# FFN weights transposed by VectorE in 32x32 blocks, in a fused gated cross-attention and FFN layer

## The chip, the cores and the metric

One core of one Trainium2 chip. The metric is the device time of one launch in microseconds (us), the median of several runs; lower is better. The engines are named PE (TensorE matmul), PEld (its weight load), DVE (VectorE), ACT (ScalarE), POOL (GpSimd) and SP (SyncE, which here only issues transfers).

## The reference

Everything is float32. x and the context are 8 batches of 128 tokens by 512.

```
x = x + tanh(g_xattn) * attention(layernorm(x), context)   # 32 heads, 8 key/value heads, D = 128, rotary positions, mask
x12 = layernorm(x) @ w12.T + b12                            # w12 is 1024 x 512, rows are outputs
x1, x2 = split(x12)                                         # 512 each
x = x + tanh(g_ffn) * ((silu(x1) * x2) @ w3.T + b3)         # w3 is 512 x 512
```

Both FFN weights are stored with outputs as rows, so the contraction axis lies along a row. The tensor engine needs it on the partitions: twelve tiles of 128x512 (eight of w12, four of w3) have to be transposed.

## The kernel before

Each float32 operand is carried as two parts, hi and lo (the rounded value and the rest), and each product is three matmuls: hi by hi, lo by hi, hi by lo (lines 468 to 470 on PE). ACT makes the hi part of a tile (L806), and DVE (L1211) or POOL (L1072) subtracts it from the source to get the lo part.

The attention runs in 32 pairs, named (gg, c) with gg 0 to 3 and c 0 to 7, p = 8 gg + c; a pair is two batches (k = 0 and 1) of one group of four heads. For each k the chain is: `scores` on PE (L591, L592) into s_banks; `mask_scores` on DVE (L1337, then four L1346), which frees s_banks; `exps` on ACT (L876, four); `recip` on DVE (L1356); `norm` on POOL (L1114); `prob_transpose` on PE (L474) into t_bank; `pT_hi_copy` on ACT and `pT_lo_split` on DVE; `pv` on PE into pv_bank; `o_hi_copy` on ACT and `o_lo_split` on DVE; `out_proj` on PE into o_bank[k]; and `add_out` on DVE (L1370), which adds to `resid`. Pairs up to (3,4) also hold two `q_block`s each, the query projections of later pairs, with which PE has other work while these chains run. The last three pairs, (3,5) to (3,7), have none.

Each engine works through its own list in order and waits on counting semaphores. The lists of pairs (3,5) to (3,7) and of what follows are written out by hand. There the layer norm of the FFN begins on DVE (`h_stats`, then the Newton steps of the inverse square root, L1225 to L1241, each of which waits for the one before), ACT normalises (`h_norm`), PE transposes the result (`h_tile`), and ACT and DVE split it (`h_copy`, `h_lo`). `up(half, m)` is the first FFN product, `down(half, b)` the second.

The twelve weight tiles are loaded by SP with one transfer each (L455), rows on partitions. `ffn_tile(t)` on PE is four 128x128 transposes through the identity into f_bank. `ffn_tile_copy(t)` on ACT copies that bank to a stage (t_cos or t_sin) and makes the hi part from the stage, `ffn_tile_lo(t)` on POOL makes the lo part. Tiles 0 to 7 stand among the instructions of pairs (3,5) to (3,7), tiles 8 and 9 after `out_proj(3,7,1)`, ahead of the first `up`, and tiles 10 and 11 between the first two `up`s.

Of the kernel before, what the change touches and what calls it, by code (L numbers as in the profile page):

```python
# [75 lines left out]
def build(nc, x, ctx, pos, mask, g_x, g_f, Wq, Wk, Wv, Wo, w12, b12, w3, b3, out):  # L76
# [1469 lines left out]
```

## Time and profile before

| | |
|---|---|
| median of 3 runs | 674.37 us (674.37 to 674.54) |
| the profiled execution | 674.48 us |
| its span | 672.7 us, so 1.8 us lie around it |
| PE busy | 661.8 us, 98%; granted clock 1.00 throughout |
| DVE, ACT, POOL busy | 482.4 us (72%), 322.0 us (48%), 385.6 us (57%) |
| chain that ended last | 90% PE, 4% DVE, 2% ACT |

A matmul's row shows its own duration, which overlaps with the next one's; what an operation takes of PE's time is read from the distance between starts. Times are from the start of the span.

### The profile page before, as it was taken

Reading aid. Unit: us, or ns where it says so; the run is one execution under the profiler, and the core shown is the slowest. Engines: PE = TensorE matmul, PEld = TensorE weight load, DVE = VectorE, ACT = ScalarE, POOL = GpSimd, SP = SyncE. Lnnn points to the kernel's source line nnn. Section 1 sums busy time; section 2 is a strip of 40 time slices with the busy share of each in tenths; the row PEclk is TensorE's granted clock in tenths of the full one; section 3 lists DMA queues with packets and bytes.
Section 4 is the critical chain, followed back from the end, with each engine's and each line's share of the span. In section 5 each row is a group of like instructions: output and inputs, shape, how many; then the busy total and the mean of one; then the engine's idle time right before and its main releaser. Section 6 shows DMA issues by size and latency. Waiting matters only on the chain.

```text
span 672.7 us, 11338 instructions
## 1 busy us (share of the span) xinstructions
PE 661.8 (98%) x3357; PEld 554.3 (82%) x3357; DVE 482.4 (72%) x1223; ACT 322.0 (48%) x903; POOL 385.6 (57%) x323
## 2 busy tenths in 40 slices
PE   8999999999999999999999999999999999999998
PEld 7888888788888888888888888888888887778886
DVE  3987666877777777777777777777777777774433
ACT  4336613554554544554554544554554537756210
POOL 6457757966666666656666666556666655631000
PEclk9999999999999999999999999999999999999999
DMA  9996982331213121321212120321211142000002
GB/s 304 317 318 215 304 295 94 142 100 58 95 39 104 32 94 33 109 71 55 94 43 98 33 94 31 110 79 45 78 33 31 32 157 80 0 1 1 1 31 95
DMA packets 62157, 66.34 MB, mean 99 GB/s; under 512 B 5920, under 2 KB 43808, under 8 KB 62112
## 3 DMA queue, kind: packets, MB, share of 16 engines
q1 hardware_dynamic: 60688, 64.77, 29.5%
q0 software_dynamic: 384, 1.05, 0.4%
q8 instruction: 18, 0.29, 0.2%
q14 instruction: 27, 0.22, 0.1%
q10 hardware_dynamic: 1040, 0.00, 0.1%
HBM read 46.93 MB, written 18.87 MB: 98 GB/s over the span
## 4 chain that ended last, share of the span: by engine, by line
PE 90%; DVE 4%; ACT 2%; issue 1%; POOL 1%; DMA 1%; SPq 0%; DVEq 0%; ACTq 0%
PE f_bank L468 11%; PE f_bank L470 11%; PE f_bank L469 11%; PE o_bank L468 9%; PE o_bank L470 9%; PE o_bank L469 9%; PE s_banks L591 6%; PE t_bank L474 4%; PE pv_bank L468 4%; PE pv_bank L470 3%; PE pv_bank L469 3%; PE s_banks L592 2%; PE t_bank L468 1%; PE t_bank L470 1%; PE t_bank L469 1%
## 5 line engine op out<-in xcount | busy, mean ns | idle before, releaser
L1114 POOL TENSOR_TENSOR prob<-prob,small 128x512 f32<-128x512 f32 x64 | 66.7, 1042 | 134.5 <-DVE small L1356 134.5
L876 ACT ACTIVATE prob<-prob,small 128x128 f32<-128x128 f32 x256 | 99.8, 391 | 80.3 <-DVE small L1346 74.9
L468 PE MATMUL o_bank<-wo_hi,o_hi 128*128 128x512 f32 x256 | 105.7, 413 | 0.0
L806 ACT ACTIVATE o_hi<-pv_bank 128x512 fp32r<-128x512 f32 x64 | 38.4, 599 | 138.1 <-PE pv_bank L470 137.7
L468 PE MATMUL f_bank<-xT_hi,wq_hi 128*128 128x512 f32 x256 | 101.5, 396 | 0.0
L470 PE MATMUL o_bank<-wo_hi,o_lo 128*128 128x512 f32 x256 | 100.5, 393 | 0.0
L469 PE MATMUL o_bank<-wo_lo,o_hi 128*128 128x512 f32 x256 | 100.0, 391 | 0.0
L1072 POOL TENSOR_TENSOR q_lo<-q,q_hi 128x512 fp32r<-128x512 f32 x64 | 82.7, 1292 | 30.0 <-ACT q_hi L806 30.0
L470 PE MATMUL f_bank<-xT_hi,wq_lo 128*128 128x512 f32 x256 | 99.8, 390 | 0.0
L469 PE MATMUL f_bank<-xT_lo,wq_hi 128*128 128x512 f32 x256 | 99.8, 390 | 0.0
L1258 DVE TENSOR_TENSOR t_sin<-f_bank,rope 64x512 f32<-64x512 f32 x128 | 88.2, 689 | 2.8
L1105 POOL TENSOR_TENSOR q<-t_cos,t_sin 128x512 f32<-128x512 f32 x64 | 82.9, 1295 | 1.0 <-DVE t_sin L1258 0.9
L1258 DVE TENSOR_TENSOR t_cos<-f_bank,rope 128x512 f32<-128x512 f32 x64 | 43.9, 687 | 32.1 <-PE f_bank L470 32.0
L1346 DVE CUSTOM_DVE_ANT_0 prob<-s_banks,prob 128x128 f32<-128x128 f32 x256 | 59.2, 287 | 10.2 <-DVE prob L1337 7.1
L591 PE MATMUL s_banks<-k_parts,q_hi 128*128 128x256 f32 x256 | 63.0, 324 | 0.7 <-issue 0.4
L1370 DVE SCALAR_TENSOR_TENSOR resid<-o_bank,small,resid 128x512 f32<-128x512 f32 x64 | 47.9, 749 | 19.6 <-PE o_bank L470 18.6
L1211 DVE TENSOR_TENSOR o_lo<-pv_bank,o_hi 128x512 fp32r<-128x512 f32 x64 | 44.1, 689 | 20.9 <-ACT o_hi L806 20.8
L470 PEld LDWEIGHTS o_bank<-wo_hi,o_lo 128*128 128x128 f32 x256 | 48.0, 188 | 11.0
L592 PE MATMUL s_banks<-k_parts,q_lo 128*128 128x128 f32 x256 | 56.9, 222 | 0.0
L470 PEld LDWEIGHTS f_bank<-xT_hi,wq_lo 128*128 128x128 f32 x256 | 48.0, 188 | 10.2
L468 PEld LDWEIGHTS f_bank<-xT_hi,wq_hi 128*128 128x128 f32 x256 | 48.1, 188 | 9.5 <-issue 0.4
L469 PEld LDWEIGHTS f_bank<-xT_lo,wq_hi 128*128 128x128 f32 x256 | 48.2, 188 | 9.1
(176 smaller groups left out, 1463.3 us busy)
## 6 DMA issues: line engine op xcount, KB each, us to landing
k_scratch<-ks_parts SPq DMA_DIRECT2D x16, 512.0 KB, 3.2
raw<-in_L_xattn_Wq_dram SPq DMA_DIRECT2D x32, 256.0 KB, 2.7
raw<-in_L_xattn_Wo_dram SPq DMA_DIRECT2D x32, 256.0 KB, 2.7
k_parts<-k_scratch SPq DMA_DIRECT2D x16, 512.0 KB, 3.7
v_scratch<-vs_hi SPq DMA_DIRECT2D x16, 256.0 KB, 3.9
v_scratch<-vs_lo SPq DMA_DIRECT2D x16, 256.0 KB, 3.9
v_hi<-v_scratch SPq DMA_DIRECT2D x16, 256.0 KB, 3.9
v_lo<-v_scratch SPq DMA_DIRECT2D x16, 256.0 KB, 4.4
```

The source lines that it names most:

```text
L468: nc.tensor.matmul(dst, st[0], mv_[0], start=start, stop=False)
L469: nc.tensor.matmul(dst, st[0], mv_[1], start=False, stop=False)
L470: return nc.tensor.matmul(dst, st[1], mv_[0], start=False, stop=stop)
L591: nc.tensor.matmul(s_banks[:, 256 * h:256 * (h + 1)], q_hi[:, k, h, :], k_parts[:, half, b, :], start=True, stop=False)
L592: mm = nc.tensor.matmul(s_banks[:, 256 * h:256 * h + 128], q_lo[:, k, h, :], k_parts[:, half, b, 0:128], start=False, stop=True)
L876: e = nc.scalar.activation(prob[:, k, h, :], prob[:, k, h, :], ACT.Exp, bias=nmin[k][:, h:h + 1], scale=-1.0, accum_out=psum_row[k][:, h:h ...
L1072: nc.gpsimd.tensor_tensor(dst, a, b_, ALU.subtract).then_inc(s, 1)
L1105: nc.gpsimd.tensor_tensor(q32[:, (e // 4) % 2, e % 4, :], t_cos[:, ts, :], t_sin[:, ts, :], ALU.add).then_inc(pool_rope, 1)
L1114: nc.gpsimd.tensor_tensor(prob[:, k], prob[:, k], rrow[k].unsqueeze(2).to_broadcast([128, GH, S]), ALU.mult).then_inc(pool_norm, 1)
L1258: return nc.vector.tensor_tensor(dst, a, b_, ALU.mult)
L1346: op = nc.vector.tensor_tensor_reduce(prob[:, k, h, :], s_parts[:, h, 0, :], prob[:, k, h, :], 1.0, HUGE, ALU.add, ALU.min, nmin[k][:, h:h ...
L1370: nc.vector.scalar_tensor_tensor(out=resid[:, b, :], in0=o_bank[k][:, :], scalar=tg_x, in1=resid[:, b, :], op0=ALU.mult, op1=ALU.add).then ...
```

## The change

The tensor engine's twelve `ffn_tile`s go, and ACT's copy to a stage with them. SP loads each tile with four transfers instead of one. Each moves 32 partitions, and each partition receives four pieces of 128 elements from four rows of the weight, chosen so that a transpose inside each 32x32 block gives the full transpose. `ffn_tile(t)` is now one DVE instruction over 128x512 (`nc.vector.transpose`), from SBUF to SBUF. ACT's `ffn_hi(t)` is one copy from its result, POOL's `ffn_lo(t)` one subtraction as before. The order of features on the partitions is a permutation, so `h_norm` writes its result permuted in the same way, and b12 is loaded in that order (eight transfers, now late in the kernel instead of at its start).

PE's order in the attention is the same without the tiles. Banks have moved: `up` uses f_bank and s_banks; `h_tile` 0 to 3 use the two halves of s_banks in turn, so `h_tile(2)` and `(3)` each wait for the split (`h_copy`, `h_lo`) of the tile two before; the outputs of pair (3,6) go to f_bank, so that `out_proj(3,7,1)` doesn't wait for an o_bank. On ACT, POOL and DVE, the lists from pair (3,2) on are written out anew. The bodies of these lists are cut here to a line or two.

```diff
-        w12_hi = cT_lo
-        w12_lo = place("w12_lo", [128, KT, TOK], F32R, at["wo_hi"])
+        w12_hi = place("w12_hi", [128, RAW, KT, 128], F32R, at["raw"])
+        w12_lo = place("w12_lo", [128, RAW, KT, 128], F32R, at["cT_lo"])
+        w12_all = place("w12_all", [128, RAW, KT, 128], F32, at["cT_lo"])
+        w3_all = place("w3_all", [128, KT, E], F32, at["wq_lo"])
...
-        up_bank = [s_banks[:, 0:512], s_banks[:, 512:1024], t_bank[:, :], pv_bank[:, :]]
+        up_bank = [f_bank[0][:, :], f_bank[1][:, :], s_banks[:, 0:512], s_banks[:, 512:1024]]
...
         def h_bank(b):
-            return (f_bank[0], f_bank[1], t_bank, s_banks[:, 0:512], *f_bank, *f_bank)[b]
+            s0, s1 = s_banks[:, 0:512], s_banks[:, 512:1024]
+            return (s0, s1, s0, s1, t_bank, pv_bank, *o_bank)[b]
+
+        def ffn_src(t, i):
+            f = slice(128 * i, 128 * i + 128)
+            if t < RAW:
+                return w12.rearrange("(h j m b) f -> h m b j f", h=2, j=4, m=4)[t % 2, t // 2, :, :, f]
+            return w3.rearrange("(t j b) f -> t b j f", t=4, j=4)[t - RAW, :, :, f]
...
-                sp.dma_start(dst, src).then_inc(s, 16)
+                for i in range(4):
+                    sp.dma_start(dst[32 * i:32 * i + 32, :].rearrange("b (j f) -> b j f", j=4), ffn_src(t, i)).then_inc(s, 16)
...
-            def ffn_tile(t):
-                src, loaded, count = ffn_tile_src(t)
-                pe.wait_ge(loaded, count)
...
-                transpose4(f_bank[t % 2], lambda k: src[:, k * 128:(k + 1) * 128]).then_inc(pe_ftile, 1)
...
             def h_tile(b):
                 pe.wait_ge(act_xn, B + b + 1)
                 if b < 2:
-                    pe.wait_ge(act_fstage, 7 + b)
-                elif b == 2:
+                    pe.wait_ge(dve_mask, 8 * KVH)
+                elif b < 4:
+                    tiles_done(H_T + b - 2)
+                elif b == 4:
...
-            for b in range(4):
-                h_tile(b)
+            h_tile(0)
+            h_tile(1)
+            h_tile(2)
+            h_tile(3)
             out_proj(3, 7, 1)
-            ffn_tile(8)
-            ffn_tile(9)
-            tiles_done(H_T + 3)
             up(0, 0)
-            ffn_tile(10)
-            ffn_tile(11)
             up(0, 1)
...
-            def ffn_tile_copy(t):
-                act.wait_ge(pe_ftile, t + 1)
...
-                hi(ffn_stage(t), f_bank[t % 2][:, :], act_fstage)
-                act.wait_ge(act_fstage, t + 1)
-                hi(ffn_tile_dst(t, 0), k4(ffn_stage(t)), act_fhi)
+            def ffn_hi(t):
+                act.wait_ge(dve_ftile, t + 1)
+                hi(ffn_parts(t)[0], ffn_f32(t), act_fhi)
...
+            exps(3, 7, 0)
             pT_hi_copy(3, 7, 0)
+            h_norm(0)
             exps(3, 7, 1)
...
+            def ffn_tile(t):
+                src, loaded, count = ffn_raw(t)
+                dve.wait_ge(loaded, count)
...
+                nc.vector.transpose(ffn_f32(t).rearrange("p k (j b) -> p k j b", j=4), src.rearrange("p (j k a) -> p k j a", j=4, k=4)).then_inc(dve_ftile, 1)
```

Three places of the new lists, as they stand before and now. The first is VectorE between `recip(3,7,0)` and the mask of `scores(3,7,1)`. Before (RECIPROCAL is `recip`, the resid row is `add_out(3,6,0)`, the last row begins the mask):

```order
L1211 TENSOR_TENSOR o_lo<-pv_bank,o_hi 128x512
L1214 BN_STATS small<-resid 128x6
L1216 BN_AGGR small<-small 128x2
L1356 RECIPROCAL small<-small 128x4
L1370 SCALAR_TENSOR_TENSOR resid<-o_bank,small,resid 128x512
L1337 TENSOR_TENSOR prob<-s_banks,mfill 128x512
```

Now:

```order
L1451 RECIPROCAL small<-small 128x4
L1326 SCALAR_TENSOR_TENSOR small<-small 128x4
L1327 TENSOR_TENSOR small<-small 128x4
L1328 SCALAR_TENSOR_TENSOR small<-small 128x4
L1326 SCALAR_TENSOR_TENSOR small<-small 128x4
L1327 TENSOR_TENSOR small<-small 128x4
L1328 SCALAR_TENSOR_TENSOR small<-small 128x4
L1336 SCALAR_TENSOR_TENSOR small<-small 128x4
L1432 TENSOR_TENSOR prob<-s_banks,mfill 128x512
```

Six Newton steps and the shift have come in between, all with both inputs in SBUF; `add_out(3,6,0)` has gone behind.

The second is GpSimd from `q_lo_split(3,7,1)` on: prob rows are `norm(3,7,0)` and `norm(3,7,1)`, w_lo rows are lo parts of weight tiles. Before:

```order
L1072 TENSOR_TENSOR q_lo<-q_61,q_hi 128x512
L1114 TENSOR_TENSOR prob<-prob,small 128x512
L1072 TENSOR_TENSOR w_lo<-t_cos,cT_lo 128x4x128
L1114 TENSOR_TENSOR prob<-prob,small 128x512
L1072 TENSOR_TENSOR w_lo<-t_sin,cT_lo 128x4x128 x2
```

Now:

```order
L1143 TENSOR_TENSOR q_lo<-q_61,q_hi 128x512
L1185 TENSOR_TENSOR prob<-prob,small 128x512
L1143 TENSOR_TENSOR w_lo<-w_all,w_hi 128x512 x3
L1185 TENSOR_TENSOR prob<-prob,small 128x512
L1143 TENSOR_TENSOR wq_lo<-w_all,wq_hi 128x4x128 x4
```

Three tiles instead of one stand between the two norms.

The third is VectorE at the start of pair (3,5), around the mask of `scores(3,5,1)`. Before, `o_lo_split(3,4,1)` stands ahead of it:

```order
L1211 TENSOR_TENSOR o_lo<-pv_bank,o_hi 128x512
L1356 RECIPROCAL small<-small 128x4
L1370 SCALAR_TENSOR_TENSOR resid<-o_bank,small,resid 128x512
L1337 TENSOR_TENSOR prob<-s_banks,mfill 128x512
L1346 ISA prob,small<-s_banks,prob 128x128
```

Now:

```order
L1451 RECIPROCAL small<-small 128x4
L1432 TENSOR_TENSOR prob<-s_banks,mfill 128x512
L1441 ISA prob,small<-s_banks,prob 128x128
L1441 ISA small 128x1
L1441 ISA prob,small<-s_banks,prob 128x128
L1441 ISA small 128x1
L1441 ISA prob,small<-s_banks,prob 128x128
L1441 ISA small 128x1
L1441 ISA prob,small<-s_banks,prob 128x128
L1441 ISA small 128x1
L1306 TENSOR_TENSOR o_lo<-pv_bank,o_hi 128x512
L1532 STREAM_TRANSPOSE w_all<-ffn_raw_95 128x4x128
```

`o_lo_split(3,4,1)` now stands behind the whole mask, and behind it one of the new transposes.

## Rows read from the trace of the kernel before

**Rows 1.** Groups by line and shape, TensorE, 555 to 615 us: busy us, mean ns; idle before

```profile
L474 PE MATMUL f_bank<-ident,raw 128*128 128x128 f32 x32 | 4.6, 275 | 0.0
...
L474 PE MATMUL f_bank<-ident,ffn_raw 128*128 128x128 f32 x16 | 2.1, 272 | 0.0
```

**Rows 2.** Timeline, TensorE: start us, duration us, instruction, idle before it

```profile
544.32 0.45 PE L468 MATMUL f_bank<-xT_hi,wq_hi 128*128 128x512 f32 x1
...
547.11 0.60 PE L474 MATMUL t_bank<-ident,prob 128*128 128x128 f32 x4
...
559.41 0.61 PE L474 MATMUL f_bank<-ident,raw 128*128 128x128 f32 x4
...
564.77 0.66 PE L474 MATMUL t_bank<-ident,prob 128*128 128x128 f32 x4 [0.23 <-POOL prob L1114]
...
571.73 0.62 PE L474 MATMUL f_bank<-ident,raw 128*128 128x128 f32 x4
...
576.90 0.66 PE L474 MATMUL t_bank<-ident,prob 128*128 128x128 f32 x4 [0.66 <-POOL prob L1114]
...
579.07 0.47 PE L468 MATMUL pv_bank<-pT_hi,v_hi 128*128 128x512 f32 x1
...
583.85 0.62 PE L474 MATMUL f_bank<-ident,raw 128*128 128x128 f32 x4
...
589.02 0.66 PE L474 MATMUL t_bank<-ident,prob 128*128 128x128 f32 x4 [0.68 <-POOL prob L1114]
...
590.02 0.47 PE L468 MATMUL o_bank<-wo_hi,o_hi 128*128 128x512 f32 x1
...
600.02 1.03 PE L474 MATMUL f_bank<-ident,ffn_raw 128*128 128x128 f32 x8
600.82 0.47 PE L468 MATMUL s_banks<-xT_hi,cT_lo 128*128 128x512 f32 x1
```

**Rows 3.** Timeline, VectorE, the last pairs and the end of the attention

```profile
557.27 0.69 DVE L1211 TENSOR_TENSOR o_lo<-pv_bank,o_hi 128x512 fp32r<-128x512 f32 x1
...
571.93 0.69 DVE L1337 TENSOR_TENSOR prob<-s_banks,mfill 128x512 f32<-128x512 f32 x1 [0.42 <-PE s_banks L592]
...
573.67 0.69 DVE L1211 TENSOR_TENSOR pT_lo<-t_bank,pT_hi 128x512 fp32r<-128x512 f32 x1
...
578.22 0.69 DVE L1211 TENSOR_TENSOR pT_lo<-t_bank,pT_hi 128x512 fp32r<-128x512 f32 x1 [0.42 <-ACT pT_hi L806]
...
582.82 0.18 DVE L1356 RECIPROCAL small<-small 128x4 f32<-128x4 f32 x1 [0.61 <-ACT prob L876]
...
584.05 0.69 DVE L1337 TENSOR_TENSOR prob<-s_banks,mfill 128x512 f32<-128x512 f32 x1 [0.42 <-PE s_banks L592]
...
598.24 0.68 DVE L1211 TENSOR_TENSOR xT_lo<-f_bank,xT_hi 128x512 fp32r<-128x512 f32 x1
```

**Rows 4.** Timeline, ScalarE, 597 us

```profile
597.56 0.60 ACT L806 ACTIVATE xT_hi<-t_bank 128x512 fp32r<-128x512 f32 x1
```

**Rows 5.** Timeline, GpSimd, 583 us

```profile
583.08 1.04 POOL L1114 TENSOR_TENSOR prob<-prob,small 128x512 f32<-128x512 f32 x1 [0.27 <-DVE small L1356]
```

**Rows 6.** Timeline, VectorE, 42 to 45 us

```profile
42.62 1.18 DVE L1231 SCALAR_TENSOR_TENSOR small<-small 128x8 f32<-128x8 f32 x1
43.84 1.21 DVE L1232 TENSOR_TENSOR small<-small 128x8 f32<-128x8 f32 x1
45.08 0.17 DVE L1233 SCALAR_TENSOR_TENSOR small<-small 128x8 f32<-128x8 f32 x1
```

**Rows 7.** Timeline, GpSimd, the same stretch

```profile
42.48 1.29 POOL L1072 TENSOR_TENSOR ks_parts<-k,ks_parts 128x512 fp32r<-128x512 f32 x1 [0.74 <-ACT ks_parts L806]
43.74 1.28 POOL L1072 TENSOR_TENSOR wk_lo<-raw,wk_hi 128x512 fp32r<-128x512 f32 x1
```

**Rows 8.** Groups by line and shape, VectorE: times, busy us, mean ns; idle before

```profile
L1214 DVE BATCH_NORM_STATS2 small<-resid 128x6 f32<-128x512 f32 x16 | 11.0, 690 | 0.3
```

**Rows 9.** Busy us by engine in pair (3,3): window, PE, PEld, DVE, ACT, POOL

```profile
525.64:540.73 15.09, 15.09 (x80) 12.77 (x78) 11.60 (x33) 7.04 (x23) 9.18 (x8) 1.00 0.11 36
```

More of the change, by code:

```diff
@@ L52 @@
 FFN_TILES = 12
+LATE = 3
 WARM = 8
@@ L674, in _ @@
                     pair(gg, c)
-            for c in range(1, 5):
+            for c in range(1, LATE):
                 pair(3, c)
@@ L728, in down @@
                 mm.then_inc(pe_down, 1)
+            q_block(3, 12)
+            scores(3, 3, 1)
+            q_block(3, 13)
+            prob_transpose(3, 3, 0)
+            out_proj(3, 2, 0)
+            pv(3, 3, 0)
+            prob_transpose(3, 3, 1)
+            out_proj(3, 2, 1)
+            scores(3, 4, 0)
+            pv(3, 3, 1)
+            q_block(3, 14)
+            scores(3, 4, 1)
+            q_block(3, 15)
+            prob_transpose(3, 4, 0)
+            out_proj(3, 3, 0)
+            pv(3, 4, 0)
+            prob_transpose(3, 4, 1)
+            out_proj(3, 3, 1)
+            scores(3, 5, 0)
+            pv(3, 4, 1)
             out_proj(3, 4, 0)
             scores(3, 5, 1)
-            ffn_tile(0)
             prob_transpose(3, 5, 0)
@@ L780, in _ @@
             up(0, 3)
-            tiles_done(H_T + 7)
             up(1, 0)
@@ L973, in _ @@
                     pair(gg, c)
-            for c in range(1, 5):
-                pair(3, c)
+            pair(3, 1)
             def h_norm(b):
@@ new lines, in _ @@
+            ffn_tile(2)
+            mask_scores(3, 3, 0)
+            ffn_tile(3)
+            ffn_tile(4)
+            recip(3, 3, 0)
+            mask_scores(3, 3, 1)
+            o_lo_split(3, 2, 1)
+            add_out(3, 1, 1)
+            cos_q(3, 12)
+            recip(3, 3, 1)
+            cos_q(3, 13)
+            pT_lo_split(3, 3, 0)
+            ffn_tile(5)
+            add_out(3, 2, 0)
+            sin_q(12)
+            pT_lo_split(3, 3, 1)
+            o_lo_split(3, 3, 0)
+            sin_q(13)
@@ new lines, in _ @@
+            mask_scores(3, 4, 0)
+            ffn_tile(6)
+            add_out(3, 2, 1)
+            cos_q(3, 14)
+            recip(3, 4, 0)
+            mask_scores(3, 4, 1)
+            sin_q(14)
+            o_lo_split(3, 3, 1)
+            cos_q(3, 15)
+            recip(3, 4, 1)
+            pT_lo_split(3, 4, 0)
+            ffn_tile(7)
+            add_out(3, 3, 0)
+            ffn_tile(8)
+            o_lo_split(3, 4, 0)
+            pT_lo_split(3, 4, 1)
+            ffn_tile(9)
+            mask_scores(3, 5, 0)
@@ new lines, in _ @@
+            sin_q(15)
+            add_out(3, 3, 1)
+            recip(3, 5, 0)
+            mask_scores(3, 5, 1)
+            o_lo_split(3, 4, 1)
+            ffn_tile(10)
+            recip(3, 5, 1)
+            add_out(3, 4, 0)
+            pT_lo_split(3, 5, 0)
+            h_stats(0)
+            add_out(3, 4, 1)
+            o_lo_split(3, 5, 0)
+            pT_lo_split(3, 5, 1)
+            mask_scores(3, 6, 0)
+            o_lo_split(3, 5, 1)
+            ffn_tile(11)
+            recip(3, 6, 0)
@@ new lines, in _ @@
+            h_stats(1)
+            mask_scores(3, 6, 1)
+            add_out(3, 5, 0)
+            pT_lo_split(3, 6, 0)
+            h_stats(2)
+            recip(3, 6, 1)
+            add_out(3, 5, 1)
+            o_lo_split(3, 6, 0)
+            h_stats(3)
+            pT_lo_split(3, 6, 1)
+            mask_scores(3, 7, 0)
+            o_lo_split(3, 6, 1)
+            inv_std_begin(0, 4, NEWTON_OPS)
+            newton_step(0, 4, NEWTON_OPS, 0)
+            recip(3, 7, 0)
+            newton_step(0, 4, NEWTON_OPS, 1)
@@ new lines, in _ @@
+            newton_step(0, 4, NEWTON_OPS, 2)
+            shifts(0, 4)
+            mask_scores(3, 7, 1)
+            pT_lo_split(3, 7, 0)
+            recip(3, 7, 1)
+            o_lo_split(3, 7, 0)
+            add_out(3, 6, 0)
+            h_stats(4)
+            pT_lo_split(3, 7, 1)
+            add_out(3, 6, 1)
+            o_lo_split(3, 7, 1)
+            h_lo(0)
+            h_lo(1)
+            add_out(3, 7, 0)
+            h_lo(2)
+            h_lo(3)
+            h_stats(5)
+            add_out(3, 7, 1)
```

411 lines of the change are left out of this document (237 added, 174 removed).

## The prediction

> **What bounds the kernel now.** I read the page first. PE is busy 98% of the span and holds 90% of the chain that ended last, so PE's time is the price of everything. The question is whether the time taken from PE is time that it needs, or time in which it waits anyway. For that I read the groups by line around the end of the attention, then PE's timeline pair by pair, then the engines that PE waits for.
>
> The groups show what goes: 48 transposes of 128x128, 6.7 us of busy time [rows 1]. By distance between starts it is less. Tiles 8 and 9 take 600.82 - 600.02 = 0.80 us together; at 0.40 to 0.46 a tile, twelve are 5.1 us [rows 2].
>
> The timeline shows where PE waits. Call S(c) the end of `scores(3,c,1)` and T(c) the start of `prob_transpose(3,c,1)`. Then T(5) - S(5) = 564.77 - 559.41 = 5.36, T(6) - S(6) = 5.17 and T(7) - S(7) = 5.17, each T with an idle time in front, released by POOL's norm [rows 2]. This stretch is a latency: mask, exps, recip, norm. The mask starts 0.20 after S and takes 1.74 (571.93 to 573.67) [rows 3]; PE's transpose comes 4.97 after the mask's start (584.05 to 589.02) [rows 2, 3]. With less work on PE it does not get shorter.
>
> **The change part by part.** The sum is made against the profiled execution, 674.48 us with a span of 672.7, 0.1 above the median of 674.37.
>
> *Tiles 0 to 7 off PE.* Tiles 0, 3 and 6 stand between S and T, so they fill a wait: worth nothing by themselves. Tiles 1, 2, 4 and 5 stand between T(c) and `pv(3,c,1)`. That product needs `pT_lo`, which starts 1.32 after T (578.22) and takes 0.69, so it can't start before T + 2.1; it does at T + 2.17 (579.07) [rows 2, 3]. Again the tiles fill a wait. Tile 7 stands between T(7) and `out_proj(3,7,0)`, which starts at T(7) + 1.0 (590.02) [rows 2]. There ACT's two copies for a tile delayed the o split, so with them gone out_proj can follow at T(7) + 0.4. Pair (3,6) gets some 0.1 longer or shorter by small moves of h_stats and the copies; I take +0.1.
>
> *The end of the attention, T(7) to the first `up`.* Before, this is 600.82 - 589.02 = 11.80 [rows 2]. Now: out_proj from 0.4 to 3.25 and pv to 3.95; `h_tile` 0 and 1 to 4.85. `h_tile(2)` has to wait until pv's result is split and `h_copy(0)` and `h_lo(0)` are through. ACT's two copies (0.5 to 0.6 each) bring it to 5.3, DVE's o split and h_lo (0.6 to 0.69 each) to 6.15 [rows 3, 4]. `h_tile(3)` waits for the next h_lo, to 6.85, and ends at 7.25; out_proj(3,7,1), 2.8, ends at 10.05. Tiles 8 and 9 no longer follow. Gain 1.75, in which tile 7 and tiles 8 and 9 are contained.
>
> *Tiles 10 and 11.* They lie between two `up`s of a PE that is busy throughout, and the layer norm and gates ahead of later `up`s have more than 2 us of room: gain 0.8, as for tiles 8 and 9.
>
> *Pair (3,5).* `o_lo_split(3,4,1)` now follows the mask of `scores(3,5,1)`. So `out_proj(3,4,1)` starts at S(5) + 0.20 + 1.74 + 0.69 + 0.1 = S + 2.75; with its 2.8 and pv's 0.7, T(5) comes at S + 6.25, against 5.36 before [rows 2, 3]: loss 0.9.
>
> *Pair (3,4).* POOL does `q_lo_split(3,5,1)` ahead of `norm(3,4,0)`. ACT's copy for it can only start when scores(3,4,1) are done; 0.2, 0.6 for ACT, 1.25 for POOL and 1.04 for the norm are 3.1, while PE has one q_block, 547.11 - 544.32 = 2.79 [rows 2, 4, 5, 7]: loss 0.3.
>
> *Pair (3,7), the largest term.* Six Newton steps and the shift stand on DVE between `recip(3,7,0)` and the mask of scores(3,7,1), all with two inputs in SBUF. At the same time POOL has norm(3,7,0), which starts 0.26 after recip (583.08 against 582.82), and now three tiles' lo parts behind it, all ready [rows 3, 5]. What that does can be read at 42 us. A Newton step that takes 0.17 took 1.18 there and ended at 43.80, as POOL's subtraction ended at 43.77; the next took 1.21, ending at 45.05 with POOL's next; with POOL idle the one after took 0.17 [rows 6, 7]. One small step passes for each POOL instruction. So, from R, the start of recip: POOL is busy from R + 0.26 to 1.3 (norm), then 3 x 1.25 to R + 5.04. Step 1 passes; steps 2 to 5 end with the four POOL instructions, the last at R + 5.05; two more at 0.2 each, and the mask starts at R + 5.5. Without the block it would be R + 1.5, which is just S(7) + 0.2, as before. Everything in front of T(7) hangs behind this mask: PE waits, and T(7) is 3.95 later.
>
> The Trainium skill, in "SBUF — State Buffer", section "Who interferes with whom", says that a VectorE instruction with two SBUF inputs and a GpSimd one that reads SBUF exclude each other for the whole instruction; the trace agrees, with 1.18 and 1.21 us in place of 0.17, and by the rule the norm and `scalar_tensor_tensor` block as well. The same section says that one with a single SBUF input outside the two-port modes does not contend; by it the new transposes would not wait for POOL. No row here shows a transpose.
>
> *The DVE transposes.* The nearest row is the instruction that reads 128x512 from SBUF alone, 0.69 us [rows 8]; I take it. The lower end is the same row less the 0.1 in which neighbours overlap, 0.6; the upper end is 0.69 plus a blocked wait of 1.2, some 1.9 [rows 6]. Ten of them fall into pairs (3,2) to (3,5), where a pair of 15.09 us leaves DVE 15.09 - 11.60 = 3.5 idle [rows 9], over three pairs 10.5. At 0.65 a slot they take 6.5: hidden behind PE's q_blocks. At 1.9 they take 19, and 3 to 8 us come onto PE. The two others stand beside exps in (3,5) and (3,6), with 1 us of room. The Trainium skill ("Vector Engine (DVE) Microarchitecture Reference", section "The reshape front-end and per-opcode configuration") has the block transpose run at one element per cycle and lane, like the row that I take; by it the sum stays.
>
> *Loads.* 48 transfers instead of 12, the first ones two pairs ahead of their use, w3's 4 to 5 us ahead: nothing, or up to 1 us where w3's second tile is late. ACT loses twelve copies that ended no wait but tile 7's.
>
> *Sum.* +0.3 (3,4), +0.9 (3,5), +0.1 (3,6), +3.95 (3,7), -1.75 (to `up`), -0.8 (tiles 10, 11) = +2.7 us. 674.37 + 2.7 = 677.1.
>
> **The rivals.**
>
> *A. The time off PE is won.* For it: 98% busy. The new order would then hide the latencies with work from elsewhere, and 5.1 us go: 669.3. Against it: the waits in front of all three T, and that PE's order has nothing new to fill them. This is the side of a faster kernel.
>
> *B. The block does not come about*, because POOL's parts fall at another moment or DVE wins the port each time. Then the mask starts when the scores are there; `h_norm(0)` in front of exps(3,7,1) costs some 0.2, and the sum is 2.7 - 3.95 + 0.2 = -1.05: 673.3. For it: the 42 us row is with two subtractions, not with a norm, and only two steps in a row were held. Against it: recip releases both engines within 0.3 us, and the three tiles are long ready. It decides as soon as less than two POOL instructions meet the steps.
>
> *C. Transposes or loads are slower than taken.* A transpose at 1.3 us, the middle of the bounds, makes 13 us in 10.5 of idle DVE, 2.5 us on top of my sum, 679.6; at the upper end up to 685. For it: no row of the operation, and the access is in runs of 32 elements. Against it: the full-width DVE rows shown, from PSUM and from SBUF, are all at 0.68 to 0.69 [rows 3, 8].
>
> **How the numbers follow.** My forecast 0.58, with its own range of 676 to 678.5 (about one POOL instruction more or less in the block, 1.25). A 0.14, B 0.16, C 0.12. A measurement of this kernel can tell about 0.2%, 1.35 us. Faster than 673.0: A, and a quarter of B, 0.18. Within: the rest of B and 0.02 of my own case, 0.14. Slower than 675.7: 0.68. The range from 672.8 to 679.8 leaves out A and half of C's upper part.
>
> **What would show it.** In the new trace: Newton steps of over 1 us between `recip(3,7,0)` and the mask, ending with POOL's instructions; the mask over 5 us after recip; T(7) - S(7) near 9; T(5) - S(5) near 6.2; T(7) to `up` near 10; transposes of about 0.69 with no PE wait in pairs (3,2) and (3,3). I am wrong if the steps stay at 0.17, or if T(c) - S(c) falls clearly below 5.1 in any pair.

## The result, and the profile after

| | before | after |
|---|---|---|
| median | 674.37 us (674.07 to 674.65, 6 runs) | 678.83 us (678.26 to 680.0, 6 runs) |
| ratio (95% interval) | | 1.0069 [1.0058, 1.0079]: slower by 0.7% |
| profiled execution, its span | 674.48, 672.7 us | 679.84, 678.0 us |
| PE busy | 661.8 us, 98% | 661.1 us, 98% |
| DVE, ACT, POOL busy | 482.4, 322.0, 385.6 us | 491.7, 315.1, 385.0 us |

4.5 us were lost where 2.7 were forecast. PE lost 48 transposes and is busy as long as before: what remained takes more of its time. Two rows of the profile's page, in 40 slices of 17 us (PE's busy tenths and its granted clock), say where:

```profile
PE   8999999999999999999999999999999998789998
PEclk9999999999999999999999999999999998979999
```

In slices 34 and 36 (559 to 576 and 593 to 610 us) the granted clock is below full, where before it was full throughout.

The new operation itself first. Groups by line, DVE, all twelve block transposes (duration in ns: lowest, median, highest):

```profile
L1532 DVE STREAM_TRANSPOSE w_all<-raw x8: 669/702/711, 511.9 to 549.3; 128x512 f32<-128x512 f32 x8
L1532 DVE STREAM_TRANSPOSE w_all<-ffn_raw x4: 701/702/703, 551.4 to 571.8; 128x512 f32<-128x512 f32 x4
```

0.70 us each, none blocked, and no wait of PE is put down to one of them: the row taken for it, 0.69 [rows 8], was right. Now PE's timeline, the instructions that answer to [rows 2] (start, duration, instruction, idle before it and its releaser):

```profile
547.23 0.66 PE L515 MATMUL t_bank<-ident,prob 128*128 128x128 f32 x4 [0.36 <-POOL prob L1185]
...
560.73 0.66 PE L515 MATMUL t_bank<-ident,prob 128*128 128x128 f32 x4 [0.98 <-POOL prob L1185]
562.31 0.53 PE L509 MATMUL o_bank<-wo_hi,o_hi 128*128 128x512 f32 x1 [0.93 <-issue]
562.64 0.63 PE L510 MATMUL o_bank<-wo_lo,o_hi 128*128 128x512 f32 x1
563.07 0.63 PE L511 MATMUL o_bank<-wo_hi,o_lo 128*128 128x512 f32 x1
...
567.42 0.60 PE L515 MATMUL t_bank<-ident,prob 128*128 128x128 f32 x4
...
579.53 0.66 PE L515 MATMUL t_bank<-ident,prob 128*128 128x128 f32 x4 [1.08 <-POOL prob L1185]
...
592.87 0.47 PE L509 MATMUL pv_bank<-pT_hi,v_hi 128*128 128x512 f32 x1 [2.92 <-issue]
...
595.23 1.11 PE L515 MATMUL t_bank<-ident,prob 128*128 128x128 f32 x4 [1.12 <-POOL prob L1185]
...
603.71 1.23 PE L515 MATMUL s_banks<-ident,xnorm 128*128 128x128 f32 x8 [1.23 <-DVE xT_lo L1306]
...
607.54 0.39 PE L509 MATMUL f_bank<-xT_hi,w_hi 128*128 128x512 f32 x1
```

T(5), T(6), T(7), the starts of `prob_transpose(3,5,1)` to `(3,7,1)`, are 567.42, 579.53 and 595.23; the first `up` is 607.54. Two things are to be seen. The wait of (3,7) is there: `pv(3,7,0)` waited 2.92 us (for `pT_lo_split(3,7,0)`, which DVE has behind the mask), T(7) another 1.12. And after a wait the matmuls follow each other at 0.43 us (562.64 to 563.07) where they do at 0.23 elsewhere. Busy time in windows (window, its length, PE, PEld, DVE, ACT, POOL, then PE's granted clock; the last two columns are DMA):

```profile
557.00:560.00 3.00, 2.75 (x17) 2.29 (x15) 2.69 (x9) 2.17 (x9) 0.36 (x1) 1.00 0.19 20
560.00:567.42 7.42, 5.76 (x19) 4.43 (x20) 5.25 (x17) 2.65 (x10) 4.18 (x4) 0.77 0.08 28
592.00:595.20 3.20, 1.24 (x3) 0.50 (x3) 1.37 (x5) 2.25 (x9) 1.06 (x2) 0.70 0.00 0
595.20:600.00 4.80, 4.77 (x14) 3.90 (x15) 3.15 (x6) 2.52 (x4) 3.47 (x3) 0.50 0.02 5
600.00:607.54 7.54, 6.31 (x35) 5.11 (x34) 4.62 (x8) 3.47 (x6) 0.25 (x1) 0.99 0.00 0
```

From 595.2 to 600 PE ran at 0.50, its lower level of 1.2 GHz; from 600 it has 2.4 GHz again. The fall itself comes earlier, inside `pv(3,7,0)`: 1.00 from 590.0 to 593.1, 0.60 in the next microsecond. So the 2.92 us wait alone stood ahead of it, and the 1.12 us wait already ran at the lower level. DVE in (3,7), answering to [rows 3, 6]:

```profile
585.14 0.18 DVE L1451 RECIPROCAL small<-small 128x4 f32<-128x4 f32 x1 [0.26 <-ACT prob L913]
585.23 0.13 DVE L1326 SCALAR_TENSOR_TENSOR small<-small 128x4 f32<-128x4 f32 x1
585.40 0.16 DVE L1327 TENSOR_TENSOR small<-small 128x4 f32<-128x4 f32 x1
585.60 0.89 DVE L1328 SCALAR_TENSOR_TENSOR small<-small 128x4 f32<-128x4 f32 x1
586.52 1.21 DVE L1326 SCALAR_TENSOR_TENSOR small<-small 128x4 f32<-128x4 f32 x1
587.77 1.22 DVE L1327 TENSOR_TENSOR small<-small 128x4 f32<-128x4 f32 x1
589.02 1.21 DVE L1328 SCALAR_TENSOR_TENSOR small<-small 128x4 f32<-128x4 f32 x1
590.26 0.16 DVE L1336 SCALAR_TENSOR_TENSOR small<-small 128x4 f32<-128x4 f32 x1
590.34 0.69 DVE L1432 TENSOR_TENSOR prob<-s_banks,mfill 128x512 f32<-128x512 f32 x1
```

and POOL beside it:

```profile
585.39 1.07 POOL L1185 TENSOR_TENSOR prob<-prob,small 128x512 f32<-128x512 f32 x1 [2.69 <-DVE small L1451]
586.43 3.78 POOL L1143 TENSOR_TENSOR w_lo<-w_all,w_hi 128x512 fp32r<-128x512 f32 x3
```

Four small steps are held, ending at 586.49, 587.73, 588.99 and 590.23, one for each of POOL's four instructions. With R the start of `recip(3,7,0)` (585.14), the mask starts at R + 5.20, forecast at R + 5.5, and then each later step of the chain has to run with PE empty.

### The profile page after: what moved, and what is told of

It is laid out like the page before. It is cut to its first block, busy times and chain, and to the rows that moved or that the text cites. A ratio compares the mean times of both kernels' runs of the same rounds, so it can differ in the third digit from the quotient of the medians.

```text
span 678.0 us, 11266 instructions
## 1 busy us (share of the span) xinstructions
PE 661.1 (98%) x3309; PEld 553.3 (82%) x3309; DVE 491.7 (73%) x1235; ACT 315.1 (46%) x891; POOL 385.0 (57%) x323
## 4 chain that ended last, share of the span: by engine, by line
PE 90%; DVE 3%; issue 2%; POOL 2%; DMA 1%; ACT 1%; DVEq 0%; POOLq 0%; ACTq 0%
PE f_bank L509 12%; PE f_bank L511 11%; PE f_bank L510 11%; PE o_bank L509 9%; PE o_bank L511 9%; PE o_bank L510 9%; PE s_banks L632 6%; PE t_bank L515 4%; PE pv_bank L509 3%; PE pv_bank L511 3%; PE pv_bank L510 3%; PE s_banks L633 2%; PE t_bank L509 1%; PE t_bank L511 1%; PE s_banks L511 1%
## 5 line engine op out<-in xcount | busy, mean ns | idle before, releaser
L509 PE MATMUL o_bank<-wo_hi,o_hi 128*128 128x512 f32 x248 | 103.8, 419 | 0.9 <-issue 0.9
L511 PE MATMUL o_bank<-wo_hi,o_lo 128*128 128x512 f32 x248 | 98.7, 398 | 0.0
L510 PE MATMUL o_bank<-wo_lo,o_hi 128*128 128x512 f32 x248 | 98.3, 396 | 0.0
L1465 DVE SCALAR_TENSOR_TENSOR resid<-o_bank,small,resid 128x512 f32<-128x512 f32 x62 | 46.4, 749 | 20.6 <-PE o_bank L511 19.7
```

The lines of the kernel that those rows point to most:

```text
L509: nc.tensor.matmul(dst, st[0], mv_[0], start=start, stop=False)
L510: nc.tensor.matmul(dst, st[0], mv_[1], start=False, stop=False)
L511: return nc.tensor.matmul(dst, st[1], mv_[0], start=False, stop=stop)
L1465: nc.vector.scalar_tensor_tensor(out=resid[:, b, :], in0=bank_of_out(gg, c, k)[:, :], scalar=tg_x, in1=resid[:, b, :], op0=ALU.mult, op1=A ...
```

## The experiments

All times below count from Z, the start of the first matmul of `scores(3,4,1)` (543.45 before, 543.05 after), in each kernel's own profiled execution; "end" is the start of PE's last matmul. "Clock" is the mean over the span. Counting from Z takes out what differs ahead of it: Z itself lies between 543.05 and 544.26 in these twelve executions, also where the program up to there is the same. A ratio compares all runs of a kernel with all runs of the kernel before beside it, so it can differ a little from the ratio of the medians.

| kernel | median (runs) | T(5) | T(6) | T(7) | `up` | end | clock |
|---|---|---|---|---|---|---|---|
| before | 674.37 (6) | 21.32 | 33.45 | 45.57 | 57.37 | 125.60 | 1.000 |
| after | 678.83 (6) | 24.37 | 36.48 | 52.18 | 64.49 | 131.36 | 0.992 |
| g_pool_moved | 673.25 (10) | 22.76 | 34.90 | 47.46 | 57.45 | 124.33 | 1.000 |
| g_o_lo_first | 678.36 (4) | 22.82 | 34.94 | 50.63 | 63.02 | 129.90 | 0.995 |
| g_fill_waits | 676.37 (5) | 22.74 | 34.87 | 50.57 | 60.58 | 127.45 | 1.000 |
| g_before_skip8 | 674.04 (10) | 21.31 | 33.08 | 44.86 | 56.66 | 124.89 | 1.000 |
| h_pair5 | 673.37 (11) | 21.91 | 34.90 | 47.45 | 57.46 | 124.34 | 1.000 |
| h_all | 672.05 (9) | 21.31 | 34.31 | 47.60 | 57.61 | 124.46 | 0.997 |
| h_newton_only | 675.17 (11) | 24.36 | 36.48 | 49.40 | 60.98 | 127.86 | 0.995 |
| h_skip12 | 673.52 (11) | 21.31 | 33.08 | 44.86 | 56.67 | 124.74 | 1.000 |
| i_split_proj | 672.33 (10) | 21.32 | 34.32 | 46.02 | 56.09 | 123.07 | 1.000 |
| i_best | 671.88 (5) | 21.31 | 33.58 | 45.73 | 56.01 | 122.99 | 1.000 |

**g_pool_moved: POOL's parts out of (3,7).**

```diff
             q_lo_split(3, 6, 0)
+            ffn_lo(4)
+            ffn_lo(5)
             q_lo_split(3, 6, 1)
+            ffn_lo(6)
             norm(3, 6, 0)
             q_lo_split(3, 7, 0)
-            ffn_lo(4)
+            ffn_lo(7)
             norm(3, 6, 1)
             q_lo_split(3, 7, 1)
             norm(3, 7, 0)
-            ffn_lo(5)
-            ffn_lo(6)
-            ffn_lo(7)
             norm(3, 7, 1)
```

> The changed kernel with one move: GpSimd's lo parts of tiles 4 to 7 stand in its idle times of pairs (3,5) to (3,6), so that none is left between norm(3,7,0) and norm(3,7,1). VectorE's list, with the Newton steps ahead of the mask, is untouched. Theory 1 (each GpSimd instruction holds one Newton step, and the long PE wait then costs TensorE's clock as well): only the norm holds a step, the mask starts 2.3 to 2.5 us after recip instead of 5.2; the wait of 2.9 us before pv(3,7,0) goes; the granted clock stays at 1.00 from there to the first up. Time 673.5 to 674.7, against 678.8 for the changed kernel. Rival 2 (the steps are slow by their place in VectorE's list, whatever GpSimd does): no change, 678.8. Rival 3 (the hold is real, but the clock falls for another reason): 675.8 to 676.5.

673.25 us (672.89 to 674.96), ratio 0.9987 [0.9977, 0.9996]: the whole loss is gone, as theory 1 has it. DVE in (3,7) now:

```profile
583.73 0.13 DVE L1326 SCALAR_TENSOR_TENSOR small<-small 128x4 f32<-128x4 f32 x1
583.90 0.16 DVE L1327 TENSOR_TENSOR small<-small 128x4 f32<-128x4 f32 x1
584.09 0.89 DVE L1328 SCALAR_TENSOR_TENSOR small<-small 128x4 f32<-128x4 f32 x1
585.02 0.16 DVE L1326 SCALAR_TENSOR_TENSOR small<-small 128x4 f32<-128x4 f32 x1
...
585.69 0.69 DVE L1432 TENSOR_TENSOR prob<-s_banks,mfill 128x512 f32<-128x512 f32 x1
```

One step is held, by the norm, and the mask starts at R + 2.05 (R = 583.64). T(6) to T(7) fell from 15.70 to 12.56. T(7) to `up` is 9.99: the 1.75 us that the forecast had expected there are found now, and not in the changed kernel, which has 12.31. That pointed to the clock.

**g_fill_waits: the same waits, filled with work.** 22 and 8 transposes of the identity, whose result nobody reads, stand in PE's two long waits.

```diff
             out_proj(3, 6, 1)
+            pe.wait_ge(act_ohi, 62)
+            pe.wait_ge(dve_olo, 62)
+            for _ in range(22):
+                nc.tensor.transpose(pv_bank[:, 0:128], ident[:, :], ident[:, :])
             pv(3, 7, 0)
+            pe.wait_ge(dve_mask, 64)
+            for _ in range(8):
+                nc.tensor.transpose(s_banks[:, 0:128], ident[:, :], ident[:, :])
             prob_transpose(3, 7, 1)
```

> The changed kernel with PE's two long waits in pair (3,7) filled: 22 extra 128x128 transposes whose result is overwritten ahead of pv(3,7,0), 8 ahead of prob_transpose(3,7,1). No wait of another engine changes. Theory (the clock fell because PE stood idle): the waits' length stays the same within 0.3 us, the granted clock from 592 to 600 us is 1.00 instead of 0.5, and the time falls by the 2.3 us that out_proj(3,7,0) and its neighbours took more: 676.5. Rival (the clock falls for another reason, or the cost of the pair lies in the waits alone): 678.8 or slightly more.

676.37 us (676.05 to 678.3), ratio 1.0043 [1.0029, 1.0058], 2.5 less than the change. The windows, columns as above:

```profile
578.34:594.04 15.70, 13.69 (x84) 11.63 (x84) 12.84 (x40) 7.09 (x23) 7.19 (x7) 1.00 0.00 1
594.04:599.00 4.96, 4.96 (x27) 4.06 (x27) 3.00 (x6) 3.34 (x6) 3.76 (x3) 1.00 0.01 2
```

T(6) to T(7) is 15.70, to the hundredth what the change has: the dependence is untouched. But the clock stays at 1.00, and T(7) to `up` is 10.01 instead of 12.31. The lower level alone costs 2.3 us there. The Trainium skill ("TensorE: Matmul & The Clock Gate", in its part on the clock gate) says that the gate follows how busy the engine has been of late and that kernels which wait between groups of matmuls swing between the two levels; the trace agrees, with 0.50 behind the empty waits and 1.00 behind the filled ones.

**g_o_lo_first: the late split of (3,5) alone.**

```diff
             recip(3, 5, 0)
+            o_lo_split(3, 4, 1)
             mask_scores(3, 5, 1)
-            o_lo_split(3, 4, 1)
             ffn_tile(10)
```

> The changed kernel with one move: VectorE's o_lo_split(3,4,1) stands between recip(3,5,0) and the mask of scores(3,5,1), no longer behind that mask. Theory: out_proj(3,4,1) then follows prob_transpose(3,5,0) at once, the granted clock stays at 1.00 there, the mask starts 0.4 later than now, and T(5) - S(5) falls from 7.8 to 5.5: 676.5. If only the wait goes and the clock still falls in this pair: T(5) - S(5) of about 7, 677.9. If o_lo_split isn't what out_proj waits for: 678.8.

678.36 us (677.88 to 678.87), ratio 1.0059 [1.0042, 1.0076]: nearly nothing, where 676.5 or 677.9 was expected. PE's timeline shows why:

```profile
565.27 0.47 PE L509 MATMUL pv_bank<-pT_hi,v_hi 128*128 128x512 f32 x1 [0.95 <-issue]
...
566.05 0.60 PE L515 MATMUL t_bank<-ident,prob 128*128 128x128 f32 x4
```

`out_proj(3,4,1)` no longer waits, and `pv(3,5,0)` waits 0.95 in its stead, for `pT_lo_split(3,5,0)`: DVE has the mask, tile 10, recip and `add_out(3,4,0)` ahead of it. T(5) is at 22.82, as in g_pool_moved (22.76), where the split is late. The 24.37 of the changed kernel has the low clock of 562 to 566 in it, and this execution and g_pool_moved's have not (1.00 there).

**h_pair5: both late values put back.** g_pool_moved with this on DVE (and on ACT `pT_hi_copy(3,5,0)` ahead of `exps(3,5,1)`, `ffn_hi(6)` behind it):

```diff
             recip(3, 5, 0)
+            o_lo_split(3, 4, 1)
             mask_scores(3, 5, 1)
-            o_lo_split(3, 4, 1)
-            ffn_tile(10)
+            pT_lo_split(3, 5, 0)
             recip(3, 5, 1)
+            ffn_tile(10)
             add_out(3, 4, 0)
-            pT_lo_split(3, 5, 0)
             h_stats(0)
```

> This is g_pool_moved with the order in pair (3,5) put back to what the kernel before had there: on VectorE o_lo_split(3,4,1) ahead of mask_scores(3,5,1) and pT_lo_split(3,5,0) straight behind it (FFN tile 10 and add_out(3,4,0) behind recip(3,5,1)), on ScalarE pT_hi_copy(3,5,0) ahead of exps(3,5,1). Theory 1 (two late values in a row, o_lo(3,4,1) for the output projection and then pT_lo(3,5,0) for the values' matmuls; g_o_lo_first freed only the first): the start of prob_transpose(3,5,1) moves from 565.89 to 565.1, and the median from 673.25 to 672.5. Rival (the wait there is set by what stands behind: recip(3,5,1) and POOL's norm(3,5,1)): prob_transpose(3,5,1) stays at 565.9 with a wait for POOL just ahead of it, and the median at 673.2.

673.37 us (672.85 to 676.03), ratio 0.9993 [0.9984, 1.0003], no better than g_pool_moved. T(5) did come 0.85 earlier than there (21.91), as the theory has it, but T(6) is where it was (34.90). PE, and behind it the row of g_pool_moved that answers to the second:

```profile
566.50 0.36 PE L632 MATMUL s_banks<-k_parts,q_hi 128*128 128x256 f32 x1 [0.62 <-issue]
568.31 0.47 PE L509 MATMUL pv_bank<-pT_hi,v_hi 128*128 128x512 f32 x1 [0.70 <-DVE pT_lo L1306]
...
578.22 0.66 PE L515 MATMUL t_bank<-ident,prob 128*128 128x128 f32 x4 [1.11 <-POOL prob L1185]
```

```profile
568.10 0.47 PE L509 MATMUL pv_bank<-pT_hi,v_hi 128*128 128x512 f32 x1 [0.75 <-DVE pT_lo L1306]
```

The gain was gone at the very next step: `scores(3,6,0)`, 0.35 behind T(5) in g_pool_moved, now waits 0.62 and starts at Z + 23.18, where it was at Z + 23.11. What it waits for is `q_lo_split(3,6,0)`, which POOL has behind `norm(3,5,1)` and ends at 566.40. The next wait, for `pT_lo_split(3,5,1)`, is no new one: `pv(3,5,1)` starts at Z + 24.99 here and at Z + 24.97 in g_pool_moved, since DVE has that split behind `h_stats(0)`, `add_out(3,4,1)` and `o_lo_split(3,5,0)` in both. So in (3,5) it is the queues of DVE and POOL that are late, not one split in them.

**h_newton_only: the other way to undo (3,7).** POOL keeps its order, DVE's steps move.

```diff
-            newton_step(0, 4, NEWTON_OPS, 1)
-            newton_step(0, 4, NEWTON_OPS, 2)
-            shifts(0, 4)
             mask_scores(3, 7, 1)
             pT_lo_split(3, 7, 0)
+            newton_step(0, 4, NEWTON_OPS, 1)
+            newton_step(0, 4, NEWTON_OPS, 2)
+            shifts(0, 4)
```

and ACT's `h_norm(0)` goes behind `o_hi_copy(3,7,0)`.

> The changed kernel with one thing undone: both Newton steps and the shift stand behind mask_scores(3,7,1) and pT_lo_split(3,7,0) on VectorE, h_norm(0) behind o_hi_copy(3,7,0) on ScalarE. POOL's ffn_lo(5), (6), (7) stay between norm(3,7,0) and norm(3,7,1). Theory 1 (the steps only cost because they stand ahead of the mask; the lo parts alone, ended at about 590.2, hardly hold norm(3,7,1)): the mask starts at R + 0.3, prob_transpose(3,7,1) at about 592.2 instead of 595.23, and since TensorE's wait there is under 2 us its granted clock stays at 1.0: median 673.5 (678.83 less 3.0 and 2.3). If the clock falls all the same: 675.8. Rival (POOL's three lo parts hold norm(3,7,1), or the Newton steps beside them hold recip(3,7,1) as long as before): prob_transpose(3,7,1) over 594, median 677.5 or more.

675.17 us (673.22 to 677.03), ratio 1.0013 [1.0002, 1.0023]. T(7) is 2.78 earlier (49.40 against 52.18; 3.0 expected), so the steps cost by standing ahead of the mask. That the clock would stay up was not right for this execution: T(7) waits 1.87 us for POOL, the clock is 0.76 from 592 to 596, and T(7) to `up` is 11.58, not 10. The three lo parts are still there; two steps meet them:

```profile
588.71 0.69 DVE L1306 TENSOR_TENSOR pT_lo<-t_bank,pT_hi 128x512 fp32r<-128x512 f32 x1
589.32 0.32 DVE L1326 SCALAR_TENSOR_TENSOR small<-small 128x4 f32<-128x4 f32 x1
589.67 1.22 DVE L1327 TENSOR_TENSOR small<-small 128x4 f32<-128x4 f32 x1
590.93 0.16 DVE L1328 SCALAR_TENSOR_TENSOR small<-small 128x4 f32<-128x4 f32 x1
```

Its eleven runs show best what the clock does to a median. Two had a mean granted clock of 1.000 and took 673.2 and 673.4; five had 0.997 and took 674.9 to 675.4; four had 0.995 and took 676.5 to 677.0. Between the groups lie some 1.8 and 1.5 us. The profiled one, of the last kind, has two stretches at the lower level, so each step is read as one such stretch, which the traces do not show for the others:

```profile
560.00:567.42 7.42, 5.51 (x21) 4.21 (x21) 5.28 (x18) 2.81 (x11) 4.54 (x4) 0.77 0.17 35
...
592.00:596.00 4.00, 2.86 (x11) 2.41 (x12) 3.52 (x6) 2.90 (x5) 3.53 (x3) 0.76 0.01 2
```

The changed kernel and this one have the fall behind 560; g_pool_moved and g_fill_waits, whose instructions up to there are the same and wait as long, have 1.00 in their profiles.

**g_before_skip8 and h_skip12: what the transposes cost before.** The kernel before, without the transposes of tiles 0 to 7, and without any of the twelve. ACT copies what lies in the banks instead, so these price PE's transposes alone; ACT's copies are still there.

```diff
-                transpose4(f_bank[t % 2], lambda k: src[:, k * 128:(k + 1) * 128]).then_inc(pe_ftile, 1)
+                if t < SKIP:
+                    pe.sem_inc(pe_ftile, 1)
+                else:
+                    transpose4(f_bank[t % 2], lambda k: src[:, k * 128:(k + 1) * 128]).then_inc(pe_ftile, 1)
```

> The kernel before, with the tensor engine's transposes of weight tiles 0 to 7 left out (it only counts the semaphore; everything behind them works on what lies in the bank, so the FFN's result is not the reference's). All other engines' lists are those of before. It prices the transposes by themselves. Theory (tiles 0 to 7 fill waits of a latency-bound stretch): 0 to 0.6 us less, 673.8 to 674.4, with the idle times in front of prob_transpose of 0.7 us grown to about 1.1 and a new one before pv(3,c,1); slower than 674.4 if the longer idle times cost clock. Rival A (PE's busy time is the time): 4.3 x 0.8, some 3.5 us less, 670.9.

674.04 us (673.35 to 674.58), ratio 0.9992 [0.9983, 1.0002]. Eight tiles, 3.4 us of PE's time, are worth 0.3, which the interval does not tell from nothing. In the profiled execution the end comes 0.71 earlier from Z. The idle times in front of T(5) to T(7) did not grow as expected (0.24, 0.48 and 0.48, before 0.23, 0.66 and 0.68); the expected new ones before `pv(3,5,1)` and `pv(3,6,1)` are there (0.58 and 0.59).

> The kernel before without any of its 12 FFN tile transposes on TensorE (4 transposes each; ScalarE copies what lies in the banks, so the FFN part of the result is not the reference's). g_before_skip8, without the first 8, gave 674.04. Theory 1 (tiles 8 to 11 stand in a stretch that TensorE itself bounds, so all of their time comes off the end): 0.8 us from the prediction's term plus what their waits cost, median 673.0, and the start of the first `up` about 0.6 earlier than the 600.92 of g_before_skip8. Rival (other waits take their place): median 674.0.

673.52 us (673.32 to 674.2), ratio 0.9989 [0.998, 0.9998]. By the medians the other four are worth 0.5, between the two theories; by the end from Z, 0.15. The trace is on the rival's side: T(7) to `up` is 11.81 with tiles 8 and 9 skipped, as with them, and two waits of PE have taken their place:

```profile
599.82 0.47 PE L469 MATMUL s_banks<-xT_hi,cT_lo 128*128 128x512 f32 x1 [0.64 <-DVE xT_lo L1215]
...
612.66 0.50 PE L469 MATMUL s_banks<-xT_hi,cT_lo 128*128 128x512 f32 x1 [0.80 <-DVE t_sin L1495]
```

So in the old order all twelve are worth 0.85 of their 5.1 us (0.86 by the end from Z; by the interval, 0.1 to 1.3).

**h_all: a version with the two undone steps and a third.** h_pair5, h_newton_only's moves, and on POOL `norm(3,4,0)` ahead of `q_lo_split(3,5,1)`.

> h_pair5 with three more moves: both Newton steps and the shift behind mask_scores(3,7,1) and pT_lo_split(3,7,0) on VectorE, h_norm(0) behind o_hi_copy(3,7,0) on ScalarE, and norm(3,4,0) ahead of q_lo_split(3,5,1) on POOL. Theory 1: the mask of (3,7,1) starts 0.3 us behind recip(3,7,0) instead of 2.05, scalar exponentials 1.25 us earlier, the 1.43 us wait of prob_transpose(3,7,1) for POOL shrinks to 0.4; pair (3,4) gives back another 0.3. Median 671.3 (h_pair5 less 1.2). Rival (h_norm late makes the h tiles late, and VectorE's steps stand ahead of o_lo(3,7,0)): what (3,7) gains comes back as a longer wait of the third h tile, 1.2 us now, and the median stays at 672.4.

672.05 us (671.84 to 673.37), ratio 0.997 [0.996, 0.998]. `prob_transpose(3,4,0)` starts at Z + 3.66 again, against 4.18 after the change. The profiled run is one with a low clock, in these windows:

```profile
580.00:582.00 2.00, 2.00 (x6) 1.52 (x6) 1.29 (x10) 0.66 (x2) 0.80 (x1) 0.50 0.00 0
582.00:584.00 2.00, 2.00 (x8) 1.59 (x6) 1.57 (x7) 1.47 (x8) 0.17 (x1) 0.65 0.00 0
```

The six runs at 1.000 or 0.999 lie at 671.84 to 672.41, three at 0.997 at 672.97 to 673.37. It beats both kernels. Against h_pair5 the median is 1.3 lower; of the runs at 0.999 and 1.000 alone, the middle one goes from 673.1 to 671.9, the 1.2 that was expected.

**i_split_proj: a wait at the end.** h_all, with TensorE's `h_tile(2)` and `h_tile(3)` in the middle of `out_proj(3,7,1)`.

```diff
             h_tile(0)
             h_tile(1)
+            out_proj(3, 7, 1, (0, 1))
             h_tile(2)
             h_tile(3)
-            out_proj(3, 7, 1)
+            out_proj(3, 7, 1, (2, 3))
```

> h_all with one more move: TensorE's h tiles 2 and 3 stand in the middle of out_proj(3,7,1), behind its first two heads (6 matmuls, 1.4 us), so that the lo part of h tile 0, for which h tile 2 waited 1.23 us, is made beside matmuls. Theory 1 (the 1.23 us was a wait that nothing covered): the time from prob_transpose(3,7,1) to the first `up` falls from 10.0 to 8.8 us, less at most 0.3 that `up` then waits for the lo part of tile 3; median 671.0 (672.05 less 1.0). Rival (`up` waits for tile 3 as long as tile 2 waited for tile 0): 672.0.

672.33 us (671.73 to 675.09), ratio 0.9979 [0.9967, 0.9991]: no gain. T(7) to `up` is 10.07, against 10.01. The 1.23 us wait is gone, but the half projection waits 0.59 (its o split is not ready), `up` 0.23, and `out_proj(3,7,0)` starts at T(7) + 0.80, where it was at + 0.41:

```profile
595.85 0.47 PE L509 MATMUL o_bank<-wo_hi,o_hi 128*128 128x512 f32 x1 [0.59 <-issue]
...
599.98 0.48 PE L509 MATMUL f_bank<-xT_hi,w_hi 128*128 128x512 f32 x1 [0.23 <-issue]
```

The rival is right in the time, not in its reason: `up` waits only 0.23 for tile 3, and the rest comes back in the two other places. T(6) to T(7), 11.70 here and 13.29 in h_all, is no gain of this move: h_all's profiled execution has its low clock there.

**i_best: h_stats out of DVE's way.** i_split_proj with `h_stats(0)` to `(3)` each one place later on DVE, so that `pT_lo_split(3,5,1)` comes 1.0 earlier; `h_stats(3)` goes behind `mask_scores(3,7,0)`.

> i_split_proj with the four h_stats of VectorE each one place later: (0) out of the way of pT_lo_split(3,5,1), into the place of (1), and so on, (3) behind mask_scores(3,7,0). Theory 1 (in pair (3,5) VectorE's queue is the limit, and the gain of h_pair5 was lost at pT_lo(3,5,1), for which pv(3,5,1) waited 0.70 us): that wait is gone, prob_transpose(3,6,1) starts 0.6 earlier against prob_transpose(3,4,0), median 670.4 (i_split_proj less 0.6). Rival (POOL's norm(3,6,1) and the exponentials hold it, whatever (3,5) does): prob_transpose(3,6,1) waits as much longer for POOL, median 671.0.

671.88 us (671.55 to 671.94), ratio 0.996 [0.9947, 0.9973], the lowest median measured. T(6) is 0.74 earlier (33.58 against 34.32), as the theory has it, but T(7) only 0.29, and `up` 0.08: `h_stats(3)` now stands in DVE's way to `recip(3,7,0)`, and `prob_transpose(3,7,0)` waits 0.87 for POOL where it waited 0.22. Its five runs all had the full clock; i_split_proj's six with the full clock lie at 671.73 to 672.38, so the two can't be told apart. Both times that were named, 670.4 and 671.0, are missed. The rival's reason is not seen, since the wait of T(6) for POOL fell from 1.11 to 0.85; the gain of (3,6) was lost in (3,7).

## Why the prediction was right in its order and short in its size

The forecast was 677.1, with more than half of the chance on 676 to 678.5, and a stated range of 672.8 to 679.8. It came to 678.83: inside the range, outside the forecast's own bounds. That it lies inside is in part luck, because the range reached so high for rival C, slow transposes, and what made the time longer was the clock, which nothing in the range stands for. Step by step, by the profiled executions:

- **(3,7), forecast 3.95: 3.58.** T(6) to T(7) went from 12.12 to 15.70. By the prediction's own measure, T(7) - S(7), it is 9.1 against 5.17, forecast near 9; S(7) came 0.4 sooner after T(6). Its R + 1.5 for the mask without the block is not what its rows give (584.05 - 582.82 = 1.23). The mechanism is shown: take POOL's parts away (g_pool_moved) or the steps from ahead of the mask (h_newton_only), and 3.1 or 2.8 us come back. That one small step passes per POOL instruction, read at 42 us [rows 6, 7], held for a norm and three subtractions. Rival B is out.
- **(3,4), 0.3: 0.5.** `prob_transpose(3,4,0)` waits 0.36 for POOL and starts 0.52 later after Z; h_all took it back.
- **(3,5), 0.9: 2.5 in the profiled execution, of which 0.9 is the order's.** T(5), counted from `prob_transpose(3,4,0)`, is 17.66 before, 20.19 after, and 18.57 where the clock stays up (g_pool_moved); T(5) - S(5) is 6.25 there, forecast 6.25. The size was right and the reason half: after `o_lo_split`, `pT_lo_split` is as late, which the forecast did not look at. Putting one back gave nothing, both 0.85 at T(5), and that was lost to the next values, `q_lo_split(3,6,0)` on POOL and `pT_lo_split(3,5,1)` on DVE.
- **(3,6), 0.1: 0.0.**
- **T(7) to `up`, forecast -1.75: +0.51.** This is the step that failed. The working is right for a TensorE at full clock: 9.99 in g_pool_moved and 10.01 in g_fill_waits, forecast 10.05. But it took the matmuls' distance from the kernel before, in a stretch that now began after 4 us of waits, and that ran at 1.2 GHz up to 600 us: 2.3 us. The prediction has no term for the clock in any of its steps.
- **Tiles 10 and 11, -0.8: -1.36** from the first `up` to the end (68.23 to 66.87). The two tiles explain 0.9 (before, 1.10 us lie between PE's starts at 606.36 and 607.46, and 0.23 where no tiles stand between); another 0.3 lies at h tiles 4 and 5 (1.43 us from 612.72 to 614.15 before, 1.10 from 618.43 to 619.53 now). The rest was not tried by itself. Nor is the 0.9 the tiles' own worth: in the old order taking them out gave 0.16 from `up` to the end (68.23 to 68.07, g_before_skip8 and h_skip12), because a wait of 0.80 came in their place.
- **The DVE transposes, hidden: right**, 0.70 us each. Rival C is out. Rival A too: without the transposes of eight tiles the old order gains 0.3 (g_before_skip8), without all twelve 0.85 (h_skip12), not 5.1.

The sum of the steps without the clock is 0.5 + 0.9 + 3.6 - 1.8 - 1.4 = 1.8, near g_fill_waits' 676.37 - 674.37 = 2.0. To this the low clock adds 2.3 at the end of (3,7) (all six runs have a mean clock of 0.995 or less), and 1.6 at 560 to 567 in two of six, by their mean clock of 0.992, which are the two near 680: with the first alone 4.1, measured 4.5 for the median. Where the other 0.4 lies stays open.

## What to carry to other kernels

Price a new wait of TensorE with what follows it, not only with its length: here waits of 4.0 us brought 2.3 us more, and filling them with transposes that nobody reads bought that back. Work that only fills a wait has no value to remove; it was worth some 0.85 of 5.1 us here, and what decides is the order in the engines that PE waits for. And when one late value is put right, read the next ones, in its queue and in the others, before a gain is promised: four of the moves here (g_o_lo_first, h_pair5, i_split_proj, i_best) mostly moved a wait to another place.

## What the runs showed of the hardware that was not expected

- The granted clock falls after some waits and not after others of the same length. In h_all's profiled run it was at 0.50 after idle times of 1.12 and 0.66 us at 577.6 and 579.8; in g_pool_moved's, with 1.13 and 0.66 at the same place, it stayed at 1.00. Two runs of one program can so differ by 1.8 us (h_newton_only), and a median over ten depends on which kind is the more frequent.
- A fall cost 1.5 to 2.3 us wherever it came: 2.3 at 593 to 600 (T(7) to `up`), 1.6 at 562 to 566 (T(5) against g_pool_moved's, from `prob_transpose(3,4,0)`), 1.8 and 1.5 between the groups of h_newton_only's runs.
- A DVE step of 0.16 us on 128x4 values, with two inputs in SBUF, is held until POOL's instruction ends, four in a row in the changed kernel: 0.89 us where it met the norm on its way, then 1.21, 1.22 and 1.21, a whole subtraction each. The block transpose, one input in SBUF, was not held in any of its twelve (0.669 to 0.711 us), with POOL busy for 12.09 of 15.0 us in pair (3,4).
